# A four-stage image kernel: the MLP, the binary convolution with the next image's first stage, and the scan's convolution written as one pipeline per engine

## The reference

```python
# L0: 8x8 patches; low = 2x2 mean, high = x - upsampled low (rolled by one row for its second half)
low  = prelu(bn(mag_w @ low));   hs = prelu(bn(phase_w @ [high, roll(high, 1)]))
x = up2(low) + hs[:, :C]
# L1: selective scan
xc, z = split(in_proj_w @ (cv1_w @ x + cv1_b));   z = silu(z)
xc = silu(depthwise3x3(xc, conv_w) + conv_b)      # "the scan's convolution"
ys = selective_scan over xc in 4 directions;  y = layernorm(sum of ys) * z
x = x + cv2_w @ (scale_w * (out_proj_w @ y)) + cv2_b
# L2: depthwise conv, layernorm, linear attention with rope, depthwise conv (cpe2), layernorm, MLP
t = t + gelu(tn2 @ fc1_w + fc1_b) @ fc2_w + fc2_b
# L3: binary convolution
y = conv3x3(sign(x), mean|w| * sign(w))
```

## Time and profile before

| | |
|---|---|
| median of 3 runs | 3729.49 us (3726.65 to 3735.41) |
| the profiled execution | 3735.58 us, of it 3733.8 us span |
| busy, of the span | PE 2960.3 us (79%), DVE 2489.9 (67%), ACT 2368.8 (63%), POOL 1090.6 (29%) |
| mean granted clock of TensorE | 0.926 of full speed |
| idle DVE before L1473, 4 images | 78.7 us, 62.7 of it waiting for POOL L702 |
| POOL L702 | 48 sums, 2365 ns mean |
| DVE L1473 | 144 taps, 1430 ns mean |
| stretch 955 to 1047 us (binary convolution with L0, image 1) | PE 87.67, ACT 69.42, DVE 56.87 us busy |
| stretch 1047 to 1063 us | PE 4.69, ACT 10.32, DVE 0.21, POOL 1.63 us busy |
| stretch 1063 to 1123 us (scan's convolution, image 1) | DVE 50.55, ACT 47.13, PE 39.91, POOL 26.91 us busy |

### The profile page before, as it was taken

How to read it: one execution, slowest core, us unless ns; L and a number is a source line. 1 busy time by engine, 2 the same in 40 slices (tenths; PEclk the granted TensorE clock), 3 DMA queues, 4 the chain that set the end, 5 groups by cost and what they waited for, 6 DMA issues and landing times. The chain is left out here.

```text
span 3733.8 us, 53627 instructions
## 1 busy us (share of the span) xinstructions
PE 2960.3 (79%) x17500; PEld 1598.4 (43%) x17500; DVE 2489.9 (67%) x2565; ACT 2368.8 (63%) x2681; POOL 1090.6 (29%) x612
## 2 busy tenths in 40 slices
PE   3678876969968877788996887776998688859699
PEld 2344334435534434434553433443554344344355
DVE  5687656875578656687466964768635896576771
ACT  2787545467678745447777864543867877454484
POOL 0235103632034500363103540146210453025530
PEclk9899997979989999898997999988999999988799
DMA  2001473600200157340020024743002004565101
GB/s 70 13 1 39 118 192 112 163 9 0 75 19 0 39 126 219 112 127 9 0 89 5 0 73 126 207 129 89 9 9 85 0 0 131 129 176 145 43 0 51
DMA packets 137195, 274.37 MB, mean 73 GB/s; under 512 B 17139, under 2 KB 93622, under 8 KB 137014
## 3 DMA queue, kind: packets, MB, share of 16 engines
q1 hardware_dynamic: 137014, 272.01, 26.4%
HBM read 194.07 MB, written 77.88 MB: 73 GB/s over the span
## 5 line engine op out<-in xcount | busy, mean ns | idle before, releaser
L1555 DVE SCALAR_TENSOR_TENSOR work<-region,cols,work 128x768 f32<-128x768 f32 x288 | 398.0, 1382 | 16.1 <-DVE work L1555 8.1
L738 POOL TENSOR_TENSOR region<-region 128x768 f32<-128x768 f32 x96 | 211.1, 2202 | 371.1 <-ACT region L919 365.4
L1075 PE MATMUL psum<-region,m_cen 128*128 128x384 f32 (+1 forms) x384 | 162.2, 548 | 171.3 <-DVE region L1669 62.3
L1075 PE MATMUL psum<-region,m_fc 128*128 128x384 f32 (+1 forms) x768 | 283.7, 493 | 10.1 <-ACT work L1026 10.1
L1323 PE MATMUL psum<-work,m_fc 128*128 128x384 f32 x768 | 282.6, 491 | 0.0
L702 POOL TENSOR_TENSOR work<-work 128x768 f32<-128x768 f32 x48 | 113.3, 2365 | 506.6 <-ACT work L839 424.5
L1473 DVE SCALAR_TENSOR_TENSOR work<-region,cols,work 128x768 f32<-128x768 f32 x144 | 202.3, 1430 | 78.7 <-POOL work L702 62.7
L1075 PE MATMUL psum<-work,m_avg 128*128 128x384 f32 x576 | 226.9, 519 | 15.1 <-ACT work L881 7.2
L277 DVE SCALAR_TENSOR_TENSOR region<-region,cols 128x768 f32<-128x768 f32 x192 | 223.9, 1166 | 19.7 <-POOL region L738 11.7
L714 POOL TENSOR_TENSOR work<-work,region 128x768 f32<-128x768 f32 x96 | 174.2, 1815 | 212.7 <-DVE work L1485 212.7
L1026 ACT ACTIVATE work<-psum,cols 128x768 f32<-128x768 f32 x192 | 173.1, 901 | 88.4 <-PE psum L1075 85.2
(11 more groups left out here) (234 smaller groups left out, 7554.5 us busy)
## 6 DMA issues: line engine op xcount, KB each, us to landing
work<-scratch_cpe SPq DMA_DIRECT2D x192, 196.0 KB, 4.1
work<-scratch_dwc SPq DMA_DIRECT2D x192, 196.0 KB, 4.1
work<-scratch_lepe SPq DMA_DIRECT2D x192, 196.0 KB, 3.9
region<-in_tab_ch SPq DMA_DIRECT2D x48, 768.0 KB, 5.2
region<-in_x SPq DMA_DIRECT2D x48, 384.0 KB, 3.3
region<-in_tab_tok SPq DMA_DIRECT2D x48, 384.0 KB, 3.2
out<-work SPq DMA_DIRECT2D x48, 384.0 KB, 2.4
scratch_cpe<-region SPq DMA_DIRECT2D x44, 392.0 KB, 4.5
```

The costliest lines, as they stand in the source:

```text
L738: g.tensor_tensor(chain_tile(conv, n, p), chain_tile(conv, n - 1, p), chain_tile(conv, n, p), ALU.add).then_inc(tap_done[n], 1)
L1075: last = pe.matmul(psum[:, bank + s, 0:HC], weights[:, :], moving(s), start=(n == 0), stop=(n == len(terms) - 1))
L1555: v.scalar_tensor_tensor(out=by_row(tile(acc + p)), in0=prow(k, b, *TAPS[n]), scalar=tap_weight(conv, TAPS[n]), in1=by_row(tile(acc + p)), ...
```

## The change

The three parts that met at the end of an image, the MLP, the binary convolution with the next L0, and the scan's convolution (now called `conv_run` and taken out of `middle`), become runs of one `overlapped` call: the MLP starts at step 0, the L0 run at step 16, the convolution at step 28. The waits that stood between the parts move into the stages that need them. SP's `load_x` of block 2 no longer waits for the whole MLP.

```diff
@@ SP
                     else:
-                        if isinstance(b, int) and b == 2:
-                            all_done(sp, i - 1, *G_ALL)
-                            sp.sem_inc(rows_seen, 1)
                         sp.wait_ge(l0_high, done(i, b - 2))
@@ ACT
             def silu_z(i):
                 def stage(b, p):
+                    if is_first(b):
+                        a.wait_ge(borders, i * 5 + 1)
                     a.wait_ge(a_mm, done(i, b))
...
-            def middle(i):
+            def conv_run(i):
...
                 def first_terms(b, p):
+                    if isinstance(b, int) and b < 2:
+                        a.wait_ge(h_store[p], i * (8 * NB) + 16)
                     a.wait_ge(a_act, done(i, following(b)))
...
-                for p in range(2):
-                    a.wait_ge(h_store[p], i * (8 * NB) + 16)
-                pipelined(a, NB, [(0, first_terms), (3, silu_u)])
+                return [(0, first_terms), (3, silu_u)]
...
-                pipelined(a, NB, [(4, gelu(0)), tap, (6, sign), (4, gelu(1)), first, second, (4, gelu(2)), (3, g_root),
-                                  (4, gelu(3)), (2, g_squares)])
-            a.wait_ge(borders, 1)
-            pipelined(a, NB, [(3, silu_z(0)), (0, relus(0))])
+                mlp = [(4, gelu(0)), tap, (6, sign), (4, gelu(1)), first, second, (4, gelu(2)), (3, g_root),
+                       (4, gelu(3)), (2, g_squares)]
+                overlapped(a, NB, [(0, mlp)] + following_runs)
+            overlapped(a, NB, [(0, [(3, silu_z(0)), (0, relus(0))]), (NB, conv_run(0))])
             with a.Fori(0, B - 1, 1) as i:
-                middle(i)
-                a.wait_ge(borders, i * 5 + 6)
-                pipelined(a, NB, [(3, silu_z(i + 1)), (0, relus(i + 1)), (0, scale_out(i, lambda p: 5))])
-            middle(B - 1)
+                middle(i, [(16, [(3, silu_z(i + 1)), (0, relus(i + 1)), (0, scale_out(i, lambda p: 5))]),
+                           (16 + NB, conv_run(i + 1))])
+            middle(B - 1, [])
@@ PE
             def l3(i, bank, lag):
                 def stage(b, p):
+                    if is_first(b):
+                        pe.wait_ge(g_x3, done(i, NB - 1))
+                        pe.wait_ge(borders, i * 5 + 5)
...
                 def l1_conv(b, p):
+                    if isinstance(b, int) and b < 2:
+                        pe.wait_ge(a_act, done(i, NB - 1))
...
-                all_done(pe, i, g_x3)
-                pe.wait_ge(borders, i * 5 + 5)
-                pipelined(pe, NB, [(3, xz(i + 1)), (0, l0(i + 1)), (0, l3(i, lambda p: 5, 1))])
+                middle(i, [(16, [(3, xz(i + 1)), (0, l0(i + 1)), (0, l3(i, lambda p: 5, 1))]), (16 + NB, conv_run(i + 1))])
@@ DVE
-                pipelined(v, NB, [(0, split), (2, join)])
+                return [(0, split), (2, join)]
-                pipelined(v, NB, [(2, scan_tap_stage(n)) for n in (2, 3, 4)])
+                return [(2, scan_tap_stage(n)) for n in (2, 3, 4)]
...
-                middle(i)
-                begin(i + 1, True)
+                middle(i, [(16, begin(i + 1, True)), (16 + NB, conv_run(i + 1))])
```

More of the change, by code:

```diff
@@ L840, in first_terms, with middle @@
                             .then_inc(signal_of, 1)
-                for p in range(2):
-                    a.wait_ge(h_store[p], i * (8 * NB) + 16)
-                pipelined(a, NB, [(0, first_terms), (3, silu_u)])
+                return [(0, first_terms), (3, silu_u)]
+            def middle(i, following_runs):
                 def soft(sweep, b, p):
@@ L1135, in l1_conv, with middle @@
                         .then_inc(b_mm, 1)
-                pipelined(pe, NB, [(3, l1_conv)])
+                return [(3, l1_conv)]
+            def middle(i, following_runs):
                 def dt(sweep, b, p):
@@ L1327, in down @@
                     return stage
-                pipelined(pe, NB, [(4, up(0)), (5, down(3)), (4, up(1)), (4, down(0)), (4, up(2)), (4, down(1)),
-                                   (3, g_variance), (4, up(3)), (4, down(2)), (2, g_centre)])
-            pipelined(pe, NB, [(3, xz(0)), (0, l0(0))])
+                mlp = [(4, up(0)), (5, down(3)), (4, up(1)), (4, down(0)), (4, up(2)), (4, down(1)),
+                       (3, g_variance), (4, up(3)), (4, down(2)), (2, g_centre)]
+                overlapped(pe, NB, [(0, mlp)] + following_runs)
+            overlapped(pe, NB, [(0, [(3, xz(0)), (0, l0(0))]), (NB, conv_run(0))])
             with pe.Fori(0, B - 1, 1) as i:
-                middle(i)
-                all_done(pe, i, g_x3)
-                pe.wait_ge(borders, i * 5 + 5)
-                pipelined(pe, NB, [(3, xz(i + 1)), (0, l0(i + 1)), (0, l3(i, lambda p: 5, 1))])
-            middle(B - 1)
-            all_done(pe, B - 1, g_x3)
-            pe.wait_ge(borders, (B - 1) * 5 + 5)
+                middle(i, [(16, [(3, xz(i + 1)), (0, l0(i + 1)), (0, l3(i, lambda p: 5, 1))]), (16 + NB, conv_run(i + 1))])
+            middle(B - 1, [])
             pipelined(pe, NB, [(0, l3(B - 1, lambda p: 5 * p, 2))])
@@ L1676, in middle @@
                 taps = [chain_tap(v, i, "cpe2", tap, 1, lambda p: chain_tile("cpe2", 2, p)) for tap in VECTOR_TAPS]
-                pipelined(v, NB, [(1, taps[0]), (1, taps[1]), (5, x3), (1, taps[2]), (1, taps[3]), (1, tap_7), (1, tap_8),
-                                  (3, g_normalise)])
-            begin(0, False)
+                mlp = [(1, taps[0]), (1, taps[1]), (5, x3), (1, taps[2]), (1, taps[3]), (1, tap_7), (1, tap_8),
+                       (3, g_normalise)]
+                overlapped(v, NB, [(0, mlp)] + following_runs)
+            overlapped(v, NB, [(0, begin(0, False)), (NB, conv_run(0))])
             with v.Fori(0, B - 1, 1) as i:
-                middle(i)
-                begin(i + 1, True)
-            middle(B - 1)
+                middle(i, [(16, begin(i + 1, True)), (16 + NB, conv_run(i + 1))])
+            middle(B - 1, [])
 def constants(S):
```

## The result

The changed kernel takes 3699.59 us (3696.27 to 3703.33, 4 runs); the kernel before took 3730.66 us beside it (3726.65 to 3735.41, 4 runs). The ratio is 0.9923, 95% interval 0.9907 to 0.9938: 0.8% faster, clear of no change. Measured once more, beside later kernels, it took 3702.98 us (6 runs), ratio 0.9932 (0.9914 to 0.995). The forecast was 3695.0, range 3685 to 3708.

The account below looks back on a forecast made before the run. No engine is full; hand-overs at two seams bound the kernel, with VectorE the bound once its taps start. Terms -36.4 + 2.1 + 0.4 + 0 - 0.6 = -34.5 us took 3729.5 to 3695.0, range 3685 to 3708.

Parts of the forecast that it names:

- First terms inside the drain: L0-to-scan-convolution seam: two blocks' `first_terms` fit ScalarE's gaps before the last `silu_z`; 9.1 us an image, 36.4 gained.
- The MLP's loops: MLP: TensorE and VectorE loop over two more steps at 0.27 us each, four images; 2.1 us lost, bounds 0 and 3.3.
- The image loop's branch: TensorE's branch between `l1_conv(11)` and the scan stays covered by the 5.35 us until `silu_u` ends; cost 0.
- rival A: Before the scan: the image branch comes bare, costing 2.6 to 7.7 us, named 3702; chance 0.11.
- The first seam: MLP to binary convolution: `l0(0)` starts as before, since `x3(11)` precedes `split(0)` on VectorE; moved waits cost 0.
- SyncE's wait: First seam: dropping the wait for the MLP ahead of block 2's load gains 0.2 us three times, 0.6.
- B: ScalarE held by the store wait, or sums not earlier; only the loops' cost is left, 3731.4 us; chance 0.06.
- C: Scan's convolution: TensorE at its low clock becomes the bound, slower, 3748 us; chance 0.03.
- the 0.4 for its loops: Scan's convolution: more blocks in TensorE's and VectorE's loops, taken 0.1 us an image, 0.4 lost.

Follow-up runs that it names:

- act_order_back: Changed kernel with ScalarE's convolution run three steps later, so all `silu_z` stand before the first `first_terms`; 3736.01 us, ratio to before 1.0016.
- one_block: Changed kernel with ScalarE's convolution run one step later, so only block 0's `first_terms` stands ahead of `silu_z(11)`; 3720.7 us, ratio to before 0.9976.
- mlp_apart: Changed kernel with the MLP written apart by the old `pipelined` list on all three engines, the other two runs still overlapping; 3704.32 us, ratio to before 0.9933.
- mlp_unrolled: Changed kernel with no hardware loop in the MLP's steps on TensorE, VectorE and ScalarE; 3695.04 us, ratio to before 0.99.
- pe_written_out: Changed kernel with TensorE's loop over images written out, so its image branch is gone; 3708.67 us, ratio to before 0.9944.
- sp_wait_back: Changed kernel with SyncE's wait for the whole MLP put back ahead of the load of x block 2; 3703.74 us, ratio to before 0.9922.
- the best kernel: Changed kernel with the MLP's steps unrolled and SyncE's output stores one step later, behind the load of x block 2; 3681.61 us, ratio to before 0.9871.
- store_lag2: Changed kernel with output stores one step later in SyncE's list, so x block 2's load precedes block 0's store; 3692.43 us, ratio to before 0.9905.
- after_beside: The changed kernel itself, unaltered, measured once more beside later kernels; 3702.98 us, ratio to before 0.9932.

## Why the prediction was right, step by step

*First terms inside the drain, 9.1 an image.* Right. The time from `silu_z(11)` to the table load fell by 9.12, 8.79, 8.69 and 7.69 us, 34.3 in all for 36.4 predicted, inside the bounds of 33.2 to 37.6. The seventh tap comes 4.03 behind `silu_z(11)` for 4.2 predicted. `silu_u(0)` came 9.9 nearer (14.52 to 4.59), not 8.8, since `l1_conv(0)` ran partly at the higher clock. `act_order_back` and `one_block` show that this step is the gain, by the mechanism given: a block's taps for each block ahead. The first image has the 9.1 to the digit; most of the 2 us short are image 3's, with 63.43 before and 55.74 now. That is in part the mark itself, which moves: in image 3 `silu_z(11)` ends 10.64 us behind the last `join` in the changed kernel, and 12.35 before. From the last `join` to the table load the four images gain 9.12, 8.95, 7.90 and 9.39 us, 35.4 in all, and image 3 the most. VectorE's wait for GpSimd fell to 34.2 rather than 40: in image 1 it is 5.24, 1.84 and 1.95 where I had 5.3, 1.9 and 2.8. (Rows 1 give the sum and the number of the four waits before and not that they were equal; they were 15.5, 16.0, 14.9 and 16.3.)

*The MLP's loops, +2.1.* The mis-sized term. `g_normalise` to `g_normalise` the four MLPs grew by 4.6 us (613.3 to 617.9), above my upper bound of 3.3. I had counted two more steps at 0.27. Three steps changed, not two: in image 0 they went from 13.73, 13.59 and 13.59 to 14.08, 14.00 and 13.72 us, 0.89 for my 0.54. And besides, in the first three images, the step in which VectorE and TensorE enter their loops went from 13.84 to 14.20, 1.1 us in all. In that step VectorE's wait ahead of `x3` is 2.65 us and was 2.31 one step earlier:

```profile
798.31 1.02 DVE L1674 SCALAR_TENSOR_TENSOR region<-psum,cols,region 128x768 f32<-128x768 f32 x1 [2.31 <-PE psum L1327]
...
812.39 1.02 DVE L1674 SCALAR_TENSOR_TENSOR region<-psum,cols,region 128x768 f32 x1 [2.65 <-PE psum L1327]
```

Image 3's MLP, which has no such step, grew by 0.60 and not by 1.3 to 1.4. The dearer entry does not come from the longer loops: `mlp_apart` has the old loops again, its later steps are back at 13.73, 13.59 and 13.59 in image 0, and its entry step still takes 14.20, which is the 1.1 us by which its MLP (614.4) is above that of before. What makes it so stays open. It was right that nothing hides the cost of these loops: `mlp_unrolled` has none there and each step is 13.59. The loops of the MLP cost 11.2 us altogether in the changed kernel, and 6.5 already before (613.3 less 606.8).

*The image loop's branch, 0.* Right, and rival A is refuted for this kernel twice, by the row (started under the first product of `l1_conv(11)`, over 1.4 us ahead of need) and by `pe_written_out`. The cover is thin, though. Of the 20 such branches in the profiles of the kernels with the change, 19 lasted 3.3 to 3.8 us and one, in image 1 of `sp_wait_back`, 5.07, as long as the cover; there the scan's first product came 0.39 us behind `silu_u(11)` and not 0.13.

```profile
L1342 PEldq COMPARE_BRANCH  x3: 76/3350/5065, 1103.9 to 2918.6; - x3
```
```profile
1109.33 1.96 PE L1077 MATMUL psum<-region,m_w_dt 128*128 128x384 f32 x4 [2.87 <-ACT region L834]
```
The Trainium skill (Advanced Engine Details and Errata, Control Flow Timing) has about 108 ns for a compare-and-branch; the trace after again disagrees for this far one, 3519 ns in the median.

*The first seam, 0 and 0.6 for SyncE's wait.* The 0.6 was nothing: 0.87 against 0.88 between the issues, and `sp_wait_back` shows no difference. I had taken the 11 us wait of the third `split` for harmless because TensorE has `l3` to do meanwhile. It was not: the late load leaves TensorE 1.8 to 2.1 us idle at `l0(2)` in every image, before and after. The change did not touch this, so the forecast did not suffer, but it is what the best kernel gains.

*Rivals B and C.* The sums do come earlier, so B is out. TensorE at its lower clock did not take over: `l1_conv` follows VectorE with 1.9 us to spare. In part it is real, though. A low stretch that meets the last two blocks costs 1.4 to 1.5 us an image (`one_block`, `store_lag2`: 6.8 to 7.2 from last tap to table load in images 1 to 3, 5.5 to 5.7 in the changed kernel).

*The sum.* By the stretches of the table the change is worth 34.3 - 4.6 = 29.7 us; the medians differ by 31.1 beside the first run of before and by 25.0 beside the later one. The forecast's 34.5 was 4.8 above this: 1.7 from the convolution (36.4 less the 0.4 for its loops, for 34.3), 2.5 from the loops, 0.6 from SyncE. The second column, 3.7 lower in the changed kernel, is left out: 1.1 of it is the mark that moves, and for the rest the other kernels with the same first seam lie between 313.4 and 316.4, so it cannot be told from the draw. The profile of the changed kernel alone (39.3 below that of before) would have hidden this; 9.2 of it is in the fourth column, where `after_beside` has 4 us more.

## What to carry to other kernels

Where a pipeline drains into the next one, look on the engine that waits in short gaps for instructions of the next pipeline that need only its first inputs; each block of the bound engine's work that is got ahead of the last hand-over is worth its whole length, here 4.7 us. A hardware loop in a chain where engines wait for each other cost a few tenths of a microsecond a step here (14.0 to 14.2 us against 13.59), which shows in no busy share. And in a queue of DMAs, put the transfer that an engine waits for ahead of the one that nobody waits for, even if the engine that waits has work: here swapping the two took about 7 us off the changed kernel, and in 3 of 30 places the idle time had brought the lower clock as well.

## What the runs showed of the hardware that I had not expected

- Steps of the MLP in which all three engines loop took 14.0 to 14.2 us where the unrolled take 13.59.
- TensorE went on at its higher clock in 27 of 27 cases after some 2 us of idle time at one place, and at the lower (pairs of 1.3 to 1.6 us instead of 0.91) in 3 of 3 after 2.8 to 3.0. That holds for this place alone: in the scan's convolution of the changed kernel the pairs went from 0.88 to 1.48 us within a block that began after 1.92 us of idle time.

```profile
1065.29 0.88 PE L1074 MATMUL psum<-region,m_dwl 128*128 x2 [1.92 <-DVE work L1473]
...
1066.89 1.48 PE L1074 MATMUL psum<-region,m_dwl 128*128 x2
```

- Leaving out a branch of 3.3 to 3.8 us moved TensorE's next product by 0.03 us (`pe_written_out`), and the median became 5.7 us longer, with intervals that overlap.
- VectorE's tap takes 2.33 us instead of 1.02 when it meets GpSimd's sum (one in three in the steady state, rows of `one_block` below), so that a block lasts 4.73 us. This agrees with the Trainium skill (SBUF — State Buffer, SBUF: two separate sides), which says that the two engines share one pair of ports and that one instruction holds it to its end.

```profile
1088.66 2.33 DVE L1473 SCALAR_TENSOR_TENSOR work<-region,cols,work 128x768 f32<-128x768 f32 x1 [0.16 <-DVE work L1473]
1091.28 1.95 DVE L1473 SCALAR_TENSOR_TENSOR work<-region,cols,work 128x768 f32<-128x768 f32 x2 [0.29 <-DVE work L1473]
1093.39 2.34 DVE L1473 SCALAR_TENSOR_TENSOR work<-region,cols,work 128x768 f32<-128x768 f32 x1 [0.16 <-DVE work L1473]
```
